# Attention with a third buffer for the probabilities, and the products with the values for two steps of keys at a time

## What is computed

```python
    def _L1_xattn_ref(x, context, w_qkv, w_proj, b_proj):
        import jax, jax.numpy as jnp
        NUM_HEADS = 16
...
        k = jnp.concatenate([extra_k, k], axis=2)
        v = jnp.concatenate([extra_v, v], axis=2)
        dtype = q.dtype
        attn = jnp.einsum('bhnd,bhmd->bhnm', q * scale, k).astype(jnp.float32)
        attn = jax.nn.softmax(attn, axis=-1).astype(dtype)
        out = jnp.einsum('bhnm,bhmd->bhnd', attn, v)
        out = out.transpose(0, 2, 1, 3).reshape(B, N, C)
        return out @ w_proj.T + b_proj
...
    x = x + jnp.tanh(g_xattn[1]) * _L1_xattn_ref(_layernorm(x, axis=-1), ctx_2048, L1_xattn_w_qkv, L1_xattn_w_proj, L1_xattn_b_proj)
```

## Time and profile before

| | |
|---|---|
| median of 3 runs | 1412.88 us (1412.67 to 1415.51) |
| the profiled execution | 1411.37 us, its span 1409.6 us |
| attention, first score to last product | about 525 to 953 us of the span |
| one group of the loop, burst to burst | 52.71 us |
| TensorE busy in it | 51.96 us |
| VectorE, ScalarE busy in it | 44.33 us, 39.70 us |

### The profile page before, as it was taken

The page is one execution under the profiler, slowest core; times in us unless marked ns, Lnnn a source line. Parts: engine busy times, 40 slices in busy tenths (PEclk is TensorE's granted clock), DMA queues, the critical chain, the costliest instruction groups (busy, mean ns, idle before and its releaser), DMA issues. The chain is left out here.

```text
span 1409.6 us, 27573 instructions
## 1 busy us (share of the span) xinstructions
PE 1139.0 (81%) x6984; PEld 749.1 (53%) x6986; DVE 763.1 (54%) x2071; ACT 587.2 (42%) x1388; POOL 320.2 (23%) x518
## 2 busy tenths in 40 slices
PE   4849999999916789999999999987449999999000
PEld 3749999999914423333233233315419888988000
DVE  6552222222254588888788788805584555555423
ACT  2622221222215407777677777783344333333000
POOL 2012222222106020101111111000013333332664
PEclk9959999999957959999999999998559999999555
DMA  5365555555347632303303303000118888887333
GB/s 173 124 222 176 176 175 184 186 182 186 109 127 190 161 74 34 48 4 46 49 1 47 48 1 47 1 1 17 44 31 240 252 256 251 253 244 231 109 108 93
DMA packets 135332, 172.73 MB, mean 123 GB/s; under 512 B 17574, under 2 KB 112800, under 8 KB 135130
## 3 DMA queue, kind: packets, MB, share of 16 engines
q1 hardware_dynamic: 119786, 132.46, 33.8%
q0 software_dynamic: 13168, 37.37, 9.1%
q10 hardware_dynamic: 2304, 2.10, 0.4%
HBM read 141.29 MB, written 30.38 MB: 122 GB/s over the span
## 5 line engine op out<-in xcount | busy, mean ns | idle before, releaser
L2035 DVE TENSOR_REDUCE arena<-ps 128x1 f32<-128x512 f32 x512 | 327.6, 682 | 69.7 <-PE ps L1876 59.5
L2006 ACT ACTIVATE arena<-ps 128x512 f32<-128x512 f32 (+1 forms) x576 | 304.1, 598 | 138.3 <-PE ps L1917 136.6
L1917 PE MATMUL ps<-arena 99*128 99x512 bf16 (+1 forms) x576 | 216.3, 388 | 6.2 <-ACT arena L2006 5.8
L1876 PE MATMUL ps<-arena 96*128 96x512 bf16 x512 | 205.7, 405 | 13.5 <-DMA arena<-k_parts 11.2
L980 POOL DMA_INDIRECT xg<-xn,tcol x134 | 127.7, 953 | 341.1 <-DVE tcol L1013 338.6
L1906 PE MATMUL ps<-arena 128*17 128x512 f32 (+1 forms) x1152 | 152.4, 601 | 2.1 <-ACT arena L2006 1.0
L1229 PE MATMUL ps<-scratch,arena 128*128 128x128 f32 x1140 | 147.8, 280 | 6.1 <-DMA arena<-in_L_ffn_w 3.6
L1917 PEld LDWEIGHTS ps<-arena 99*128 99x128 bf16 (+1 forms) x576 | 56.9, 101 | 178.5 <-ACT arena L2006 141.0
L1071 PEld LDWEIGHTS ps<-scratch,arena 128*128 128x128 f32 x1248 | 147.9, 195 | 3.6 <-issue 1.7
L1071 PE MATMUL ps<-scratch,arena 128*128 128x128 f32 x1248 | 148.4, 278 | 1.1 <-ACT scratch L1102 1.1
L1229 PEld LDWEIGHTS ps<-scratch,arena 128*128 128x128 f32 x1140 | 136.4, 194 | 12.6 <-issue 11.7
(11 more groups left out here) (310 smaller groups left out, 1263.4 us busy)
## 6 DMA issues: line engine op xcount, KB each, us to landing
arena<-in_L_ffn_W SPq DMA_DIRECT2D x47, 1024.0 KB, 5.1
arena<-in_L_ffn_w SPq DMA_DIRECT2D x190, 192.0 KB
y<-ysb SPq DMA_DIRECT2D x95, 128.0 KB
arena<-k_parts SPq DMA_DIRECT2D x48, 137.6 KB, 5.1
arena<-q_parts SPq DMA_DIRECT2D x96, 64.0 KB, 5.4
scratch<-y SPq DMA_DIRECT2D x16, 256.0 KB, 2.9
arena<-in_L_ffn_w POOLq DMA_DIRECT2D x8, 512.0 KB, 10.0
xg<-xn,tcol POOLq DMA_INDIRECT x134
```

The source lines that it names most:

```text
L1876: nc.tensor.matmul(ps[:, MAXB + pos % NMAXB, :], e.q_aug[u][0:QROWS, c, h, t * P:(t + 1) * P], e.k_aug[u][0:QROWS, h, CL + k * HB:CL + (k ...
L1917: nc.tensor.matmul(ps[0:rows, SB + n % NSB, :], e.k_aug[u][0:AROWS, h, k0:k0 + rows], e.q_aug[u][0:AROWS, c, h, :], start=True, stop=True) ...
L2006: nc.scalar.activation(e.prob[s % 2][0:rows, h, :], ps[0:rows, SB + (s * GH + h) % NSB, :], ACT.Exp).then_inc(p_ready, 1)
L2035: v.tensor_reduce(e.mx[:, c, h, t, k:k + 1], ps[:, MAXB + pos % NMAXB, :], AX.X, ALU.max).then_inc(max_done, 1)
```

## The change

The probabilities get a third buffer (`NPROB = 3`), and room for it is made by starting the attention's buffers at the place of a ring of weights (`ATT0 = W13_1`) that only the last mixture of experts loads, in a later block. The products with the values are called in other steps: `weighed_at(s)` gives the steps whose probabilities are taken in step s. That is nothing in odd steps of the first half and in even steps of the second, two steps at once in steps 2, 4, 6, 8 and 11, 13, 15, 17, and one in steps 0 and 9. A group of 18 steps then has 2 single bursts and 8 double ones. The place within the step is the same, between the scores of heads 1 and 2. The waits of the exponentials are put one step earlier to match the third buffer.

```diff
-ATT0 = W13_1 + RING1 * W13_BYTES
+ATT0 = W13_1
...
-    prob1 = buf([GH, HB])
+    prob1 = [buf([GH, HB]) for _ in range(NPROB - 1)]
...
-    e.prob = [buf([GH, HB]), prob1]
+    e.prob = [buf([GH, HB])] + prob1
...
+NPROB = 3
...
+    def weighed_at(s):
+
+        c, n = divmod(s, MT)
+        if n == 0:
+            return [s - 1] if c else []
+        return [s - 2, s - 1] if n % 2 == 0 else []
+
...
-                    ins = nc.tensor.matmul(ps[h * 32:h * 32 + HD + 1, AB, :], e.v_g[u][0:rows, mt, h, :], e.prob[s % 2][0:rows, h, :],
+                    ins = nc.tensor.matmul(ps[h * 32:h * 32 + HD + 1, AB, :], e.v_g[u][0:rows, mt, h, :], e.prob[s % NPROB][0:rows, h, :],
...
-                    if s > 0:
-                        weigh(g, u, s - 1)
-                    elif not first:
+                    for done in weighed_at(s):
+                        weigh(g, u, done)
+                    if s == 0 and not first:
                         weigh(g - 1, 1 - u, STEPS - 1)
...
-                        if h == 0 and not (isinstance(g, int) and g == 0 and s < 2):
-                            act.wait_ge(pv_done, g * STEPS + (s - 1))
-                        nc.scalar.activation(e.prob[s % 2][0:rows, h, :], ps[0:rows, SB + (s * GH + h) % NSB, :], ACT.Exp).then_inc(p_ready, 1)
+                        if h == 0 and not (isinstance(g, int) and g == 0 and s < NPROB):
+                            act.wait_ge(pv_done, g * STEPS + (s - NPROB + 1))
+                        nc.scalar.activation(e.prob[s % NPROB][0:rows, h, :], ps[0:rows, SB + (s * GH + h) % NSB, :], ACT.Exp).then_inc(p_ready, 1)
```

## The result

The changed kernel takes 1429.84 us (median of 4 runs, 1425.58 to 1432.87) against 1412.78 us (4 runs, 1411.13 to 1415.51): the ratio is 1.0125, with an interval of 1.0102 to 1.0147. That is 17.7 us slower by the ratio (14.4 to 20.8 by its interval), and 17.1 by the medians; 21.8 were forecast.

The account below looks back on a forecast made before the run. TensorE was taken as the bound, busy 51.96 of 52.71 us per group. Six loop groups +17.9, group 7 +2.3 and group 0 +1.6 made +21.8 us on 1411.4: 1433 us, range 1416 to 1446.

Parts of the forecast that it names:

- (a): Two steps with eight maxima: the last maxima wait for VectorE's reductions to free three banks, +0.53 us, 22 places.
- (b): Two steps with turned maxima (4 to 6, 13 to 15): TensorE waits for GpSimd's chain from `row_max`, +0.87 us.
- The drain: TensorE's array change, not paid by a pair's second burst: 0.2 us less in each of 64 double bursts, 12.8 us.
- The case in which no drain is saved: Rival: each burst of a pair needs its own change of the array, 12.8 us more, 1446 us; chance 0.1.
- (d): Group 7 past its maxima: TensorE waits for ScalarE's exponentials, +0.22 us in each of five pairs; whole group +2.3.
- (c): Six or seven maxima, no turn: steps 0 to 2 and 9 to 11 gain 0.2 us each, 6 to 8 nothing.
- the clock falls: Rival: longer gaps bring one to four more stretches of lowered TensorE clock, 1437 to 1446 us; chance 0.08.
- group 0: First turn in step 7, its chain covered by the double burst; with its other stretches +1.6 us, an estimate.
- Only the drain is saved: Rival: reductions and GpSimd's chain fit anyway, only the array changes are saved, 1399 us, faster; chance 0.1.
- only the chain bites: Rival: only GpSimd's chain and ScalarE hold TensorE, the maxima are never held, 1417 us; chance 0.08.

Follow-up runs that it names:

- the split pair: The changed kernel with the score of head 2 put between the two bursts of a pair; ratio 1.0236 to the kernel before.
- the kernel with pairs and half reductions: The changed kernel with each reduction of the maxima reading only 256 of the 512 columns; 1398.99 us, ratio 0.9919 to the kernel before.

## Why the prediction came out as it did

The forecast was 1433 us, +21.8; measured were 1429.84 us, +17.7 by the ratio. The mechanisms of (a) and (b) are those that the runs show. That the total came so near is in part luck: the profile has some 1.4 us less of ScalarE's waits than the sum, 3 us more of half-rate clock and other stalls, and 4.9 us less behind the attention, where nothing should have moved.

**The drain.** Forecast 1.86 us from a double burst to the next score, measured 593.71 to 595.56, 1.85. So the second burst of a pair pays no change of the array, and the split pair shows what one costs, 0.22 us. The case in which no drain is saved falls. Of the 64 places, the five of group 7 hide the gain behind ScalarE, as (d) has it.

**(a) Eight maxima.** Forecast 6.35 us, measured 6.34; the waits lie at the sixth to eighth maximum, and shorter reductions take them away. 22 such places forecast: in the groups of the loop all three per group have 6.33 to 6.34.

**(b) The turn.** Forecast 600.21 - 593.09 = 7.12, measured 602.66 - 595.56 = 7.10 (7.11 to 7.13 in most groups); the turn placed behind the burst takes the wait away. The prediction put TensorE's stall there at 1.6 us; it is 1.2 (1.39 less 0.22), since the fifth maximum, too, is held by its bank on the way (598.33, 0.43 us late) and eats part of the wait. The sum doesn't hang on it.

**(c) and (d), ScalarE.** Here a term was mis-sized. The prediction took 0.60 us for the exponential that opens a step. That row's exponential had in fact waited for its score. The row beside it, four exponentials over a step's opening in 2.06 us, already had 0.49 throughout, and the two readings contradict each other. With 0.49 the fifth exponential ends 0.1 us earlier: steps 6 to 8 take 5.46 instead of 5.57 us and gain 0.14 against the 5.59 of before, in place of nothing, and two steps of group 7 take 5.20 instead of 5.32 in its last three pairs. The term of the sum that was mis-sized is thus ScalarE's wait in steps 6 to 8 and in group 7: 7 x 0.11 and 5 x 0.12, 1.4 us too much. A group of the loop comes to +2.8 (55.5 us in the undisturbed ones; group 1 has one turn 0.1 us longer) where +3.0 was forecast.

**The clock.** The case "the clock falls" held in part. In the profile of the changed kernel the double burst of step 6 ran at half rate in groups 3, 5 and 7, as this one of group 5 (TensorE in order of time, with the ordinary burst of step 4 ahead):

```profile
823.26 1.91 PE L1914 MATMUL ps<-arena 128*17 128x512 f32 x16
...
829.50 0.23 PE L1897 MATMUL ps<-identb,arena 128*128 128x128 bf16 x1 [1.02 <-POOL arena L1826]
830.37 3.60 PE L1914 MATMUL ps<-arena 128*17 128x512 f32 x16
```

Each of the three comes right behind the long wait at the turn, and costs 1.1 to 1.7 us: the stretch with the turn takes 8.6 us instead of 7.11 in group 3 and 8.8 in group 5. A fourth half-rate stretch of this kernel has nothing to do with a turn. It lies in group 5 as well, in step 1, behind the stall of 1.2 us at the return of the loop:

```profile
813.43 0.63 PE L1884 MATMUL ps<-arena 96*128 96x512 bf16 x1
813.86 0.63 PE L1925 MATMUL ps<-arena 99*128 99x512 bf16 x1
...
816.41 0.57 PE L1884 MATMUL ps<-arena 96*128 96x512 bf16 x1
```

At full clock a maximum or score is listed with 0.38 and the next one starts 0.22 us behind it, not 0.43. This stretch costs 1.5 us (steps 0 to 2 take 9.3 us here, and 7.8 in group 3, which has the same stall at full clock). The kernel before has one, at the same place in group 3, longer and 3.3 us dear:

```profile
690.50 0.63 PE L1876 MATMUL ps<-arena 96*128 96x512 bf16 x1
691.06 1.91 PE L1906 MATMUL ps<-arena 77*17 77x512 f32 x8
```

So half rate costs 5.7 us after (1.5, 1.7, 1.5 and 1.1) against 3.3 before, a net 2.4 us. The prediction had this as a rival at 3.3 us and more, and not in the walked sum. It judged by group 7's row that the trace of before shows no swing of the clock; the 0.94 of group 3 is one. Whether the wait at the turn brings the clock down is open. For it speak the places, and that none of the kernels with the turn behind the burst shows a half-rate burst behind a turn in its profile. Against it, the kernel with pairs and half reductions is idle for 0.9 to 1.2 us ahead of each of its 14 turns and has no such burst behind one; the kernel with split pairs has one such burst. These are one profile of each kernel.

**The sum.** The attention grew by 23.4 us in the profile. The six groups of the loop without their disturbances make 6 x 2.8 = 16.9 (forecast 17.9), group 7, from its single burst to its last score, without its half-rate burst 3.0 - 1.1 = 1.9 (forecast 2.3), group 0 1.4 (forecast 1.6): 20.2 in place of 21.8. The half rate adds the net 2.4, and the stalls at the loop's return, 2.1 us each where they were 1.9, with the longer turn of group 1 some 0.5: that is 23.1, and 0.3 are left over. The runs' difference of 17.7 is less than the profile's attention, as the stages around vary by a few us from execution to execution. "Only the drain is saved" and "only the chain bites" fall: both (a) and (b) are needed, and each kernel that removes one of them keeps the other's waits.

## What to carry to other kernels

Before a burst on a busy engine is made longer and rarer, count what the others must take between two bursts: with three banks, a consumer that was paced by the short bursts falls behind in the long gap and idles in the long burst, though its total load doesn't change. A fixed chain through another engine that ran under one of the removed bursts becomes a wait, unless its consumer is placed behind the next one. And a spacing read from one pair of rows should be checked against a longer run of the same instruction: here the difference was an instruction that waited for its input.

## What was not expected of the hardware

TensorE's clock fell to half for little more than one double burst (830.37 to 833.9 us) and between 530 and 950 us TensorE was never idle for as much as 1.3 us at a time; the granted clock of the group's stretch then reads 0.97, or 0.94 where there are two such falls. An idle time of 1.0 to 1.3 us in otherwise dense work goes ahead of each of the four in the changed kernel, three at a turn and one at the return of the loop. But the other eleven turns have idle times of 0.7 to 1.0 us there too, and no such burst behind them.
